# Token sums T3, T2, T1 moved from GpSimd to VectorE, with new orders and bank-by-bank copies, in a Strassen-Winograd residual MLP kernel

## What is computed

```python
s0 = relu(x @ swi[0]) @ swo[0]            # 512 -> 2048 -> 512
s1 = relu(x @ swi[1]) @ swo[1]
eo = relu(x @ wi[label]) @ wo[label]      # one expert per sequence
w  = softmax(relu(concat(eo[0], s0[0], s1[0]) @ g1) @ g2)   # from the first token of a sequence
x  = x + eo * w[0] + s0 * w[1] + s1 * w[2]
x  = x + x @ W[category] + b[category]    # one 512 x 512 matrix per sequence
```

## Time and profile before

| | |
|---|---|
| median of 3 runs | 1981.06 us |
| profiled execution, its own time | 1979.77 us |
| its span, first to last instruction | 1978.0 us |
| mean granted TensorE clock | 0.995 |
| TensorE busy (matmuls) | 1940.1 us, 98% |
| VectorE busy | 1334.8 us, 67% |
| ScalarE busy | 981.7 us, 50% |
| GpSimd busy | 547.9 us, 28% |

### The profile page before, as it was taken

The page is one execution under the profiler, slowest core; times in us unless marked ns, Lnnn a source line. Parts: engine busy times, 40 slices in busy tenths (PEclk is TensorE's granted clock), DMA queues, the critical chain, the costliest instruction groups (busy, mean ns, idle before and its releaser), DMA issues. The chain is left out here.

```text
span 1978.0 us, 25205 instructions
## 1 busy us (share of the span) xinstructions
PE 1940.1 (98%) x8504; PEld 1598.5 (81%) x8504; DVE 1334.8 (67%) x1381; ACT 981.7 (50%) x1438; POOL 547.9 (28%) x408
## 2 busy tenths in 40 slices
PE   6999999998999999999999999999989999999998
PEld 5788888886888888888888888888878888888886
DVE  6888788898566565555755554589885665555565
ACT  5665766665453443344554444466555533344342
POOL 5546545654121111111311111244641111111120
PEclk9999999999999999999999999999999999999999
DMA  5666667766876666666776676578768776656642
GB/s 218 239 258 262 261 256 284 281 244 245 292 245 213 214 212 213 192 194 197 240 258 205 194 223 205 190 277 293 274 207 262 244 234 211 218 186 212 217 157 93
DMA packets 187026, 450.99 MB, mean 228 GB/s; under 512 B 16916, under 2 KB 57876, under 8 KB 180500
## 3 DMA queue, kind: packets, MB, share of 16 engines
q1 hardware_dynamic: 186900, 449.39, 67.3%
HBM read 308.81 MB, written 140.51 MB: 227 GB/s over the span
## 5 line engine op out<-in xcount | busy, mean ns | idle before, releaser
L1339 PE MATMUL ups<-XH,WU 128*128 128x512 f32 x2688 | 888.2, 391 | 22.1 <-DVE WU L1000 8.1
L1339 PE MATMUL rps<-HH,WD 128*128 128x512 f32 x2672 | 881.2, 391 | 11.6 <-DVE ACC L1039 7.3
L1339 PEld LDWEIGHTS ups<-XH,WU 128*128 128x128 f32 x2688 | 506.3, 188 | 134.6 <-DVE hid L1061 9.3
L1339 PEld LDWEIGHTS rps<-HH,WD 128*128 128x128 f32 x2672 | 503.8, 189 | 119.8 <-DVE ACC L1039 8.1
L1339 PE MATMUL ups<-XL,WU 128*128 128x512 f32 x1344 | 524.4, 390 | 0.0
L1339 PE MATMUL rps<-HL,WD 128*128 128x512 f32 x1336 | 521.5, 390 | 0.0
L612 POOL TENSOR_TENSOR HT<-hid 128x512 f32<-128x512 f32 x96 | 132.1, 1376 | 928.5 <-PE rps L1339 928.5
L1020 DVE TENSOR_TENSOR HL<-HT,HH 128x1024 fp32r<-128x1024 f32 x240 | 306.0, 1284 | 9.2 <-ACT HH L809 5.1
L1339 PEld LDWEIGHTS ups<-XL,WU 128*128 128x128 f32 x1344 | 253.3, 188 | 51.9
L1339 PEld LDWEIGHTS rps<-HL,WD 128*128 128x128 f32 x1336 | 252.1, 189 | 52.3
L1042 DVE SCALAR_TENSOR_TENSOR ACC<-rps,gw,ACC 128x1024 f32<-128x1024 f32 x126 | 161.4, 1281 | 192.0 <-PE rps L1339 191.8
(11 more groups left out here) (114 smaller groups left out, 1623.5 us busy)
## 6 DMA issues: line engine op xcount, KB each, us to landing
WU<-wu_kept SPq DMA_DIRECT2D x448, 256.0 KB, 3.4
WD<-wd_kept SPq DMA_DIRECT2D x224, 512.0 KB, 3.3
wd_kept<-WD SPq DMA_DIRECT2D x112, 512.0 KB, 3.0
wu_kept<-WU SPq DMA_DIRECT2D x32, 1024.0 KB, 4.9
wu_kept<-WU SPq DMA_DIRECT2D x32, 768.0 KB, 4.3
sums_kept<-ACC SPq DMA_DIRECT2D x28, 512.0 KB, 5.5
MB<-sums_kept SPq DMA_DIRECT2D x28, 512.0 KB, 5.5
PUR<-in_L_cond_swi_dram SPq DMA_DIRECT2D x16, 512.0 KB, 6.0
```

The lines of the kernel that those rows point to most:

```text
L1339: ins = pe.matmul(dst, stationary[a], moving[c], start=start and j == 0, stop=stop and j == 2, skip_group_check=True)
```

## The change

Five things are changed. T3, T2 and T1 of the next block are made by VectorE at all three ends (GpSimd makes none), and the low parts and adds near them change places. At the start, T1 is made first, directly after the first low part, the up weights' late low parts come ahead of token low parts 2 and 3, and ScalarE's high parts are made in the order 0, 4, 1, 2, 3, 6, 5. `x_sum_count` gives the counts that fit the new order. TensorE waits for the copies of the first down product bank by bank. In the tail, the last down product goes into rps[0], begun anew, and is added after the sixth, and the banks of the output products are taken in another order.

```diff
+LAST_ANEW = [True, False, True, False, False, False, True]
...
-X_HI_FIRST = [0, 3, 1, 2, 6, 4, 5]
+X_HI_FIRST = [0, 4, 1, 2, 3, 6, 5]
+X_SUM_FIRST = [0, 2, 3, 1]
+X_SUM = [0, 1, 2, 3]
+def x_sum_count(s, q):
+    return 3 * s + (X_SUM if s > 0 else X_SUM_FIRST)[q]
...
             elif which == 2:
+                for j in (0, 1):
+                    eng.wait_ge(s_xs[j], 16 * (s + 1))
                 dst, p, q, op = XT[:, 4, :], XS[:, 1, :], XS[:, 0, :], ALU.subtract
...
-        tail_banks = [aps[:, :], ups[2], rps[0][:, 0, :], rps[0][:, 1, :], ups[0], ups[1], rps[1][:, 0, :], rps[1][:, 1, :]]
+        tail_banks = [aps[:, :], ups[2], ups[0], ups[1], rps[1][:, 0, :], rps[1][:, 1, :], rps[0][:, 0, :], rps[0][:, 1, :]]
...
# GpSimd, loop over m
-                if end:
-                    token_sum(pool, super_of(m) + 1, 0)
-                    token_sum(pool, super_of(m) + 1, 1)
                 if N < STEPS:
                     hidden_sum(pool, N, 0, 0)
                     hidden_sum(pool, N, 0, 1)
-                if end:
-                    token_sum(pool, super_of(m) + 1, 2)
...
# ScalarE, before and in m = -1
-            token_high(0, 3)
+            token_high(0, 4)
...
                     token_high(0, 2)
-                    token_high(0, 6)
+                    token_high(0, 3)
...
-                    token_high(0, 4)
+                    token_high(0, 6)
                     token_high(0, 5)
...
# VectorE, before the loop
             token_low(0, 0)
+            token_sum(dve, 0, 2)
             up_low(0, 0)
             token_sum(dve, 0, 0)
             token_sum(dve, 0, 1)
             token_low(0, 1)
-            token_sum(dve, 0, 2)
+            up_low(0, 1)
             token_low(0, 2)
             token_low(0, 3)
-            up_low(0, 1)
             token_sum(dve, 0, 3)
...
# VectorE, loop over m
                     up_low(b + 1, 0)
+                if end:
+                    token_sum(dve, s + 1, 0)
+                    token_sum(dve, s + 1, 1)
                 second(4)
...
                 block_22(b)
+                if end:
+                    token_sum(dve, s + 1, 2)
                 hidden_low(N, 0)
                 mix(1, 1)
                 second(5)
...
                     token_low(s + 1, 2)
+                out_part(1, 1)
+                if not end:
+                    made(m, 5)
+                second(6)
+                if end:
                     token_low(s + 1, 3)
-                out_part(1, 1)
-                made(m, 5)
-                if end:
+                    made(m, 5)
                     token_low(s + 1, 4)
-                second(6)
...
# VectorE, tail
             hidden_low(t0, 4)
             tail_low(0)
-            last_add(4, 1, pair, 3)
             hidden_low(t0, 6)
+            last_add(4, 1, pair, 3, True)
+            last_add(5, 3, rps[1], 2, True)
             tail_low(1)
-            last_add(5, 3, rps[1], 2)
+            last_add(5, 2, rps[1], 0, False)
             tail_low(2)
-            last_add(6, 2, rps[1], 0, 0)
-            last_add(6, 2, rps[1], 0, 1)
+            last_add(6, 2, rps[0], 6, True, 0)
+            last_add(6, 2, rps[0], 6, True, 1)
...
# TensorE, down(N, p)
                 if N < STEPS - 1:
-                    if i in (1, 2):
-                        pe.wait_ge(s_pc, 2 * (N + 1))
...
                 else:
-                    if p == 1:
-                        pe.wait_ge(s_pc, 2 * (N + 1))
...
+                    anew = LAST_ANEW[p]
                     if p >= 4:
-                        pe.wait_ge(s_tadd, p - 2 + (p == 6))
+                        pe.wait_ge(s_tadd, (2, 3, 1)[p - 4])
                     if i in (3, 5):
                         dst = ups_all[:, 0:2, :]
+                    if i == 6:
+                        dst = rps[0]
...
                 for j in range(2):
                     cols = slice(j * P, (j + 1) * P)
+                    if i in (1, 2):
+                        pe.wait_ge(s_pc, 2 * N + 1 + j)
...
# TensorE, output products
-                if q == 6:
-                    pe.wait_ge(s_tadd, 7)
+                if q in (2, 4, 6):
+                    pe.wait_ge(s_tadd, {2: 4, 4: 6, 6: 8}[q])
```

More of the change, by code:

```diff
@@ L582, in token_sum @@
                 eng.wait_ge(s_xs[0], 16 * (s + 1))
-                eng.wait_ge(s_xT, 3 * s + 1)
+                eng.wait_ge(s_xT, x_sum_count(s, 1))
                 dst, p, q, op = XT[:, 2, :] if s > 0 else first_T2, XT[:, 1, :], XS[:, 0, :], ALU.add
             elif which == 2:
+                for j in (0, 1):
+                    eng.wait_ge(s_xs[j], 16 * (s + 1))
                 dst, p, q, op = XT[:, 4, :], XS[:, 1, :], XS[:, 0, :], ALU.subtract
@@ L588, in token_sum @@
                 eng.wait_ge(s_xs[3], 16 * (s + 1))
-                eng.wait_ge(s_xT, 3 * s + 2)
+                eng.wait_ge(s_xT, x_sum_count(s, 2))
                 dst, p, q, op = XT[:, 5, :], XT[:, 3, :], XT[:, 2, :], ALU.subtract
@@ L682, in _ @@
                 rel = m % STEPS_SUPER
-                end = m >= 0 and rel == STEPS_SUPER - 2 and super_of(m) < SUPERS - 1
                 if d >= 0:
@@ L713, in token_high @@
                 if sums:
-                    act.wait_ge(s_xT, 3 * s + sums)
+                    act.wait_ge(s_xT, x_sum_count(s, sums))
                 elif fourth:
@@ L976, in _ @@
             for n, (j, h) in enumerate(TAIL):
-                act.wait_ge(s_tadd, (1, 4, 5, 6, 7)[n])
+                act.wait_ge(s_tadd, (1, 4, 5, 7, 8)[n])
                 act.activation(tail_part(XH, j, h), tail_part(XT, j, h), ACT.Copy).then_inc(s_thi, 1)
@@ L987, in token_low @@
                 if sums:
-                    dve.wait_ge(s_xT, 3 * s + sums)
+                    dve.wait_ge(s_xT, x_sum_count(s, sums))
                 if fourth:
@@ L1282, in _, with last_add @@
             t0 = STEPS - 1
-            def last_add(p, j, src, count, h=None):
+            def last_add(p, j, src, count, last, h=None):
                 g = GATE_PART[NETS - 1]
-                last = p in (1, 4, 5, 6)
                 toks = slice(0, TB) if h is None else slice(2 * P * h, 2 * P * (h + 1))
@@ L1313, in _ @@
             hidden_sum(dve, t0, 1, 2)
-            last_add(1, 0, rps[0], 0)
+            last_add(1, 0, rps[0], 0, True)
             hidden_low(t0, 2)
-            last_add(2, 3, pair, 0)
+            last_add(2, 3, pair, 0, False)
             hidden_low(t0, 5)
-            last_add(3, 1, rps[1], 0)
+            last_add(3, 1, rps[1], 0, False)
             hidden_low(t0, 4)
             tail_low(0)
-            last_add(4, 1, pair, 3)
             hidden_low(t0, 6)
+            last_add(4, 1, pair, 3, True)
+            last_add(5, 3, rps[1], 2, True)
             tail_low(1)
-            last_add(5, 3, rps[1], 2)
+            last_add(5, 2, rps[1], 0, False)
             tail_low(2)
-            last_add(6, 2, rps[1], 0, 0)
-            last_add(6, 2, rps[1], 0, 1)
+            last_add(6, 2, rps[0], 6, True, 0)
+            last_add(6, 2, rps[0], 6, True, 1)
             tail_low(3)
```

## The result

The changed kernel takes 1970.67 us (median of five runs, 1969.35 to 1972.2) against 1981.06 for the kernel before (five runs, 1980.32 to 1982.97): the ratio is 0.9949, 95% interval 0.9937 to 0.9961, so 10.4 us or 0.5% faster. The profiled executions took 1979.77 and 1970.03 (spans 1978.0 and 1968.2), 9.7 us apart. Forecast were 1973.4 with a range of 1965 to 1978, and 0.84 for faster. The size is near; the term for the start is far off, and the two bad ends came out unequal.

The account below looks back on a forecast made before the run. TensorE was taken as the bound, stalling at the first and third block ends where weights are still prepared. Start -0.3, bad ends -3.6, copies -0.2 and tail -3.6 sum to -7.7: 1981.06 becomes 1973.4 us, range 1965 to 1978.

Parts of the forecast that it names:

- the term for the start: Start of the kernel: first up product later, about 11.2, but TensorE resumes at 27.45 instead of 27.75; -0.3 us.
- bad ends: Ends of the first and third token blocks, where TensorE stalls: -1.8 us each, -3.6 together, bounds -3.4 to -0.2 each.
- 9.2 - 3.6: In a bad end: GpSimd's eight operations take 9.2 us, about 3.6 beside VectorE's PSUM operations; the other 5.6 are lost turns.
- between 0 and 0.9, I take 0.4: In a bad end: cost in us of matmuls running at 1.2 GHz behind the wait for u.
- behind that point the shift is handed on one for one: At the start, after TensorE resumes at 27.45: each step waits for TensorE, so the -0.3 us carries unchanged to 60 us.
- The tail: End of the kernel: the 2.85 us wait for XT goes and outputs start at 1949.25, not 1952.87; -3.6 us.
- The -0.6 for product 1: In the tail: last step's product 1 starts at 1932.5 instead of 1933.08, one copy of 0.58 sooner.
- Copies: First down product's copies awaited bank by bank, so down product 1's first half needs only the first copy; -0.2 us.
- Rival C: Waits inside 96 products expose a 0.19 us weight load each, 18.2 us; total +10.5, 1991.6 us; chance 0.04.
- The second end: End of the second token block: TensorE's own matmuls cover VectorE's added work; cost 0, or 1.15 us if cover is gone.
- A: Rival: VectorE does not feel GpSimd's turns, each bad end gives back its 9.5 us; 1958 us, chance 0.08.
- B: Rival: VectorE's additional 3.45 us eats the idle 3.81 us, ends give 0; total -4.1, 1977.0 us, chance 0.17.

Follow-up runs that it names:

- the move alone: Kernel before with only T3, T2, T1 moved to VectorE at the block ends, adds in old order; bad ends gave 0.7 and 2.0 us, tail 58.2 us.
- the order alone: Kernel before with only one down-product add put ahead of VectorE's low parts 3 and 4 at block ends; first and third end each lost 0.5 us.
- T1 twice: Changed kernel with a second, redundant T1 made by VectorE at each token block's end; span 1973.3 us.
- the kernel with the longer transfer wait: Changed kernel with the last step's hidden sum 3 of half 1 on GpSimd instead of VectorE; span 1968.9 us, tail 53.4 us.
- the ends alone: Kernel before with only the block ends changed: T3, T2, T1 on VectorE and one add ahead of low parts 3 and 4; span 1974.4 us.

## Why the prediction was right, and which steps were off

**The bad ends: right in mechanism and in the sum of both, off in each.** Forecast: VectorE 2.2 us sooner (measured 2.4 at the first end, 3.5 at the third), product 5 held by u through 5.15 us of ScalarE (476.10 to 481.21: 5.1), a wait of about 4 us for it (3.6), one of about 0.9 for XL3 (0.5), one of about 1.0 for block 22 (0.9 at the first end, none at the third). The stretches of 38 us hold 130 and 140 matmuls, where 134 to 140 were expected. The sum of both, -3.6, was -3.4. But the first end gave 0.3 (-1.8 forecast) and the third 3.1, both inside the bounds of -3.4 to -0.2. Two terms make the difference. The first is a turn won or lost, 1.1 us: the forecast counted turns as 9.2 - 3.6 and did not say at which instruction they fall; the runs show one at T3, lost where GpSimd started 0.14 us ahead, and one at low part 3, saved by the new order. The second is "between 0 and 0.9, I take 0.4" for the low clock behind the wait for u. The shifts behind product 5 show what it was: 1.9 us at the first end (-5.02 to -3.11), 0.4 to 0.7 at the third. The 1.9 lay above the bound that I had given. I had argued that block 22 of the next step was late anyway; with VectorE sooner it was so no more (487.6, while TensorE came at 489.56). That the sum of both ends is so near is luck in part: an end with a turn lost at T3 and a long stretch at 1.2 GHz stands beside one with no such turn and a short stretch.

**The start: right sign, size wrong.** -0.3 was forecast, -3.2 found in the profile. By steps: the first product 11.06 (11.2 forecast), but by another way than I said. T1 could start only at 8.45; it let the sum at 8.24 pass and delayed GpSimd's fourth (1.59 us), and the first low part of the weights waited for T1 and for that sum. Release by block 22 at 27.08 (27.45 forecast). Up to there -0.67. The failed step is "behind that point the shift is handed on one for one": behind a wait of 1.0 us TensorE stayed at 2.4 GHz where before, behind 2.83 us, it had fallen to 1.2 (27.75 0.80 in the earlier trace rows); that made it -2.0 by the next wait, at 38.30. The changed kernel, and then the windows of the kernel before and of the move alone, which has the old start:

```profile
27.08 0.50 PE L1351 MATMUL ups<-XH,WU 128*128 128x512 f32 x1 [1.00 <-DVE hid L1066]
```

```profile
27.00:33.00 6.00, 5.25 (x17) 4.24 (x18) 1.29 (x3) 2.68 (x5) 0.00 (x0) 0.72 0.32 131
```

```profile
27.00:33.00 6.00, 5.46 (x24) 4.52 (x25) 2.32 (x4) 3.96 (x7) 0.00 (x0) 1.00 0.32 131
```

The third row shows that the low clock does not belong to the old order: behind the same wait of 2.83 us the clock stayed at 2.4 GHz with the move alone, and also with the order alone. Later in the first step there is another wait, of 4.3 us in both kernels, and the low clock behind it lasted less long: -3.2. I had this in the lower bound (-2.5), not in the sum.

How much of it is the change's: at the first full group the seven kernels with the new start stood at -2.0, -2.3, -3.0, -3.1, -3.2, -3.3 and -3.7 (mean -2.95), the six with the old one at +0.5, +0.4, 0, -1.2, -2.5 and -2.7 (mean -0.9). So the start is worth about 2.0 us in the mean, and the profile before was on the slow side. The runs split it in three. TensorE resumes behind block 22 at 26.8 to 27.4 us with the new start and at 27.5 to 28.1 with the old one: 0.7 us in the mean, the only part that the forecast worked out. From there to the next wait it is 11.2 to 11.3 us in all seven new ones and in two of the old, and 12.6 to 12.8 in the other four of the old, where the clock fell. And from the wait at 50 us to the first full group it is 5.6 to 7.0 us with either start, as the stretch at 1.2 GHz is shorter or longer.

**The tail: -3.6 forecast, -2.7.** The wait for XT went, as worked out. The -0.6 for product 1 was wrong: I took the releaser in the row at its word, and VectorE's low part ended in the same 0.1 us. The other 0.3 is that the output products did not follow at once: the first began at 1943.00, 0.5 us behind the start of the last matmul of the down products, when the second low part was ready (1941.63 + 1.22).

**Copies: -0.2 forecast, at most -0.3,** and nothing at the bad ends, as said. Rival C (waits inside products cost) is refuted: full groups are 5.44 us apart in both kernels.

**The second end: 0 forecast, -0.5** in the change, and up to +0.7 in one execution, because VectorE's queue now waits for the transfer; this wait I had not looked for. The forecast's "VectorE waits for TensorE there" was true, and there is slack left, some 2.6 us: where the hidden sum came 3.0 us later (T1 twice, and the kernel with the longer transfer wait), product 5 waited 0.35 and 0.43 us for u.

**Rivals.** A (no turns felt, 1958) and B (ends give nothing, 1977) are out: T3, T2 and T1 show their lost turns, and the ends alone gained 5.7 us together. That the total came within 2.7 us of the forecast owes something to errors of both signs: in the profiles the start gave 2.9 us more than forecast and the second end 0.5 more, the tail 0.9 less, and the bad ends and the copies each 0.2 less.

## What to carry to other kernels

Before an operation is moved to another engine's queue, lay out that queue up to the instruction that releases the bound engine, with the turns that it loses to the other engine and the instruction at which each falls; and follow the time that it frees through every later wait, since here most of a removed wait of 3.6 us came back as one for another operand. Compare the traces group by group, not by spans: the stages' gains here differed by up to 3 us from one execution to the next, with opposite signs that a total hides. When a row names a releaser, look for whatever else ended in the same 0.1 us before costing its removal.

## What was not expected of the hardware

The clock that TensorE is granted after a short wait differs between executions and places with the same wait: behind 2.85 us in the tail it stayed at 2.4 GHz once and fell to 1.2 five times (tail 56.6, 58.2 to 59.4 us); behind 3.6 us it was 0.54 over 6.5 us at one end and 0.74 at the other; behind 2.67 us 0.74 at both. The Trainium skill ("TensorE: Matmul & The Clock Gate", What's actually happening) describes a monitor that is not in step with the kernel, which would make the same wait come out in different ways; the runs agree as far as these numbers go, and nothing here shows the monitor itself.
